# Row maxima copied into the score banks, and the low key products of two tiles side by side

## The chip, the cores and the metric

One core of a Trainium2 chip runs the whole program in one launch. The metric is the time on the device in microseconds (us), as the median of the runs shown.

## The reference

The reference is two small layers on 1024 tokens of width 128 with a context of 6404 rows. The change lies in the first of them, the cross attention. Cut to what matters:

```python
def _L0_xattn_ref(x, latents, ..., Wq, Wkv, Wout):     # 16 heads of 64
    x, lat = layer_norm(x, ...), layer_norm(latents, ...)
    q = lat @ Wq                                       # 1024 queries
    k, v = split(concat([x, lat], axis=1) @ Wkv)       # 6404 + 1024 = 7428 keys
    dots = einsum('bhid,bhjd->bhij', q, k) * scale
    attn = softmax(dots, axis=-1)
    out = einsum('bhij,bhjd->bhid', attn, v)
    return out @ Wout
```

Everything is float32 in the reference. The kernel keeps that accuracy with 16-bit operands: queries, keys, values and probabilities are each held as a high part and a low part, and the products of the parts that matter are added up.

## The kernel before, in words

`stage_attention` takes most of the time. It works head by head (16), for each head over two halves of 512 queries, and in a half over 59 tiles of 128 keys: 58 full ones and a last short one. Two tiles make a unit (30 units a half, 60 a head), and two units, so four tiles, make a period (`PERIODS` = 30 a head, w = 0 to 29). Period 14 holds the last full unit and the short tile of the first half, period 15 begins the second half, and likewise 29 and 0.

For each tile n:

- TensorE (`score`) writes scores, 128 keys by 512 queries, into bank `S[n % 3]`, with two matmuls of 512 columns over all 128 rows. The first multiplies the high keys, held twice (`kc`), with the high and the low part of the queries (`qc`). The second multiplies `kd` with `qd`: its upper 64 rows hold the low keys and the high queries, its lower 64 rows a constant 1/64 and the negated row maximum of the queries, so that the maximum is subtracted inside the matmul.
- ScalarE (`exp`) turns the bank into probabilities in SBUF (one of three buffers of a unit, `prob`), and frees the bank.
- GpSimd (`head` of its block) takes the low part of a whole unit's probabilities, 128 by 1024, into one of three `prob_low`. It waits for both exponentials of the unit and for `low_done` of the unit three earlier.
- TensorE multiplies the high part with the values (`apply_high`: 8 matmuls of 64 or 65 columns a tile) and, two units later, the low part (`apply_low`: 4 matmuls a tile, 8 a unit). All of it adds up in one bank `O`.

Woven into the same order, written out by hand, are two other jobs:

- The maxima of the next head. In each period `window` makes four score products with only 64 rows each (high keys and high queries), in two pairs. The two of a pair stand in different halves of the array. They go to banks `X[0]` to `X[3]`, and VectorE (`take`) reduces them pair by pair to their maxima. A program of 30 windows is offset by 12 periods against the head. Twice a head (w = 13, 27) the maxima of one half are spread over a bank (`spread_top`), and ScalarE writes them negated into `qd` (`place_top`).
- The projections of the next pair of heads. In `side`, TensorE projects 512 columns of queries or keys, or four tiles of values, into `Y`, which is `X[0]`. ScalarE copies the high part out (`copy_task`), VectorE subtracts for the low part (`split_task`), and SyncE writes both to memory, from which whole heads are loaded later (`load_kq`, `load_v`). An even head has 17 such periods (queries and keys: 0, 2, ..., 28 and 9, 19), an odd one 15 (values, all within w = 0 to 22). Heads 14 and 15 have none.

`side` may write `Y` only when the first pair's `take` is done, and the next `window` only when the side's last reader is done (`side_read`). So the order of a projecting period is a loop through bank `X[0]`: window, take, projection, copy, split, window.

In the order of `head` before, a middle period from its window on is: the second tile's `apply_high` of the even unit, a `score`, an `apply_low`; then the odd unit's first `apply_high`, a `score`, the `side`, the second `apply_high`, a `score`, an `apply_low`; then the first `apply_high` of the next period and a `score`, and the next window. Each `score` is three tiles ahead.

Of the kernel before, what the change touches and what calls it, by code (L numbers as in the profile page):

```python
# [18 lines left out]
P = 128  # L19
# [295 lines left out]
def stage_attention(nc, pers, A):  # L315
# [5 lines left out]

    sc = Scope(nc, "att", pers.whole)
    with sc:
# [14 lines left out]
        ident_h = sc.sb("ident_h", [P, P], F16)  # L338
        rden = sc.sb("rden", [P, 4])
# [13 lines left out]
                 "max_scored max_taken top_ready top_spread top_placed inverted normalized tail_ready v_ready kd_ready ident_ready").split()  # L353
# [3 lines left out]
         v_ready, kd_ready, ident_ready) = (s[n] for n in names)  # L357
# [64 lines left out]

        def unit_of(n):
# [14 lines left out]
        def _(sp):  # L438
# [35 lines left out]

            def load_kq(m):
                e = m % 2
                sp.dma_start(kc[0:DH, e, 0:KEYS], k_high[rows(m), :]).then_inc(k_in[e], 16)
                sp.dma_start(kc[DH:P, e, 0:KEYS], k_high[rows(m), :]).then_inc(k_in[e], 16)
                sp.dma_start(qc[0:DH, e, :], q_high[rows(m), :]).then_inc(q_in[e], 16)
                sp.dma_start(qc[DH:P, e, :], q_low[rows(m), :]).then_inc(q_in[e], 16)  # L480
                sp.dma_start(qd[DH:P, e, :], q_high[rows(m), :]).then_inc(q_in[e], 16)
                sp.dma_start(kd[DH:P, e, 0:KEYS], k_low[rows(m), :]).then_inc(k_in[e], 16)

# [18 lines left out]
            sp.dma_start(kd[DH:P, 0, 0:KEYS], k_low[rows(0), :]).then_inc(k_in[0], 16)  # L502
            for b in range(HEADS):
                i, e = divmod(b, 2)
                projecting = i + 1 < HEADS // 2
                for w in range(PERIODS):
                    if w == 0 and b + 1 < HEADS:
                        if b:
                            sp.wait_ge(scored, b * HEAD_TILES)
                        if b and e:  # L510
                            for r in range(NR):
                                sp.wait_ge(kq_out[r], kq_writes(i + 2, r))
                        load_kq(b + 1)
# [74 lines left out]
        def _(pe):  # L588
# [26 lines left out]
            def window(m, e, k, turn):  # L615


                if k == 0:
                    pe.wait_ge(q_in[e], 48 * (turn + 1))
                    pe.wait_ge(k_in[e], 48 * (turn + 1))  # L620
# [29 lines left out]
            def next_score(b, g, i):  # L650
                n = place(b, g, i) + 3
                if n < HEADS * HEAD_TILES:
                    score(n)
# [45 lines left out]
            def side_read(b, e, w, projecting, i):  # L699
# [4 lines left out]
                elif w == BACK_AT:  # L704
                    pe.wait_ge(top_placed, 2 * b + 2)
                elif w == FRONT_AT:
                    pe.wait_ge(top_placed, 2 * b + 3)
# [10 lines left out]
            def head(b, e, with_max, projecting, i):  # L718
                for g in range(UNITS):
                    p, w = g % SIDE, g // 2  # L720
                    if p == 0:
                        next_score(b, g, 0)
                        if g:
                            apply_low(b, e, g - 2)
                        elif b:
                            apply_low(b - 1, 1 - e, LAST - 1)
                        next_window(b, e, w, with_max, projecting, i)
                        if g:
                            apply_low(b, e, g - 1)
                        elif b:  # L730
                            apply_low(b - 1, 1 - e, LAST)
                        next_score(b, g, 1)
                        clear_sums(b, e, g, i)
                        apply_high(b, e, g, 0)
                        apply_high(b, e, g, 1)
                        continue
                    apply_high(b, e, g, 0)
                    next_score(b, g, 0)
                    if g % 2:
                        side(b, e, w, with_max, projecting, i)  # L740
                    else:
                        next_window(b, e, w, with_max, projecting, i)
                    if p < PAIRS:
                        apply_high(b, e, g, 1)
                        next_score(b, g, 1)
                    if p >= 2:
                        apply_low(b, e, g - 2)

# [34 lines left out]
            pe.wait_ge(k_in[0], 48)  # L783
            for n in range(3):
                score(n)
                for x in (66 + 2 * n, 67 + 2 * n):
                    first_slot(x)
# [6 lines left out]
        def _(act):  # L794
# [40 lines left out]

            def head(b, e, with_max, projecting, i):
                for g in range(UNITS):
                    w = g // 2
                    for x, _ in tiles(g):
                        if place(b, g, x) + 3 < HEADS * HEAD_TILES:  # L840
                            exp(place(b, g, x) + 3)
                        n = task_at(e, w) if projecting else None
                        if g % 2 == 0 or x:
                            pass
                        elif n is not None:
                            copy_task(i + 1, n)
                        elif w == BACK_AT:
                            place_top(b, e, 1)
                        elif w == FRONT_AT and with_max:
                            place_top(b + 1, 1 - e, 0)  # L850
# [29 lines left out]
            for n in range(3):  # L880
# [5 lines left out]
        def _(dve):  # L886
# [34 lines left out]

            def finish_max(m, half):
# [13 lines left out]
            def head(b, e, with_max, projecting, i):  # L936
                for w in range(PERIODS):
# [7 lines left out]
                    if n is not None:  # L945
                        split_task(i + 1, n)
                    if 2 * w + 2 in (SIDE, UNITS):
# [787 lines left out]
```

## Time and profile before

| | before |
|---|---|
| median of 3 runs | 2514.27 us (2513.64 to 2515.91) |
| the profiled execution | 2518.84 us, span 2517.0 us |
| TensorE clock granted, mean | 0.98 |
| windows of the maxima, first to last | 122.0 to 2066.1 us of the span |
| TensorE matmul busy | 2375.0 us (94%) |
| GpSimd busy | 1860.1 us (74%) |
| VectorE busy, ScalarE busy | 1580.7 us (63%), 1506.1 us (60%) |

How to read it: the profiled execution is one of its own, 4.57 us above the median of the others, and durations come from it. Its span leaves out what lies around the program. Matmuls are pipelined: a matmul of 512 columns shows a duration of 0.38 us while the next starts 0.215 us after it, so starts are compared, not busy times.

### The profile page before, as it was taken

The numbers are of one execution on the slowest core, as the hardware profiler recorded it, in microseconds if no ns is written. First come the engines' busy times: TensorE is split into PE (matmuls) and PEld (weight loads), VectorE is DVE, ScalarE is ACT, GpSimd is POOL, SyncE is SP. The second block draws the span as 40 slices with busy tenths as digits, with TensorE's granted clock in tenths as the row PEclk, the third lists the DMA queues.
The fourth block names the chain that finished last, engine by engine and source line by source line (L and its number), as shares of the span: only waits on it lengthen the run. The fifth ranks groups of instructions, "written<-read, shape, count | busy, mean of one in ns | idle before, by whom it ended". The sixth has DMA issues, their size and how long they took to land. (4 is left out here: it accounts for less than half of the span.)

```text
span 2517.0 us, 77679 instructions
## 1 busy us (share of the span) xinstructions
PE 2375.0 (94%) x33657; PEld 1488.4 (59%) x33657; DVE 1580.7 (63%) x2342; ACT 1506.1 (60%) x2589; POOL 1860.1 (74%) x1105
## 2 busy tenths in 40 slices
PE   2999999999999999999999999999999998779996
PEld 1355665566556655665566556655665565558884
DVE  8866666666666666666666666666666650467854
ACT  4666666666665666666666666666666665146642
POOL 1788888888888888888888888888889999120001
PEclk9899999999999999999999999999999999889988
DMA  2611323131413141314131413141313000510000
GB/s 86 156 39 45 80 70 103 37 92 61 112 35 90 60 113 40 89 60 113 35 89 64 109 39 90 63 110 38 86 54 99 2 2 7 166 31 2 2 2 12
DMA packets 94102, 162.79 MB, mean 65 GB/s; under 512 B 9976, under 2 KB 83648, under 8 KB 88640
## 3 DMA queue, kind: packets, MB, share of 16 engines
q1 hardware_dynamic: 90464, 153.71, 21.8%
q8 instruction: 265, 4.34, 0.7%
q10 hardware_dynamic: 3296, 4.10, 0.5%
q14 instruction: 77, 0.63, 0.1%
HBM read 95.81 MB, written 61.97 MB: 63 GB/s over the span
## 5 line engine op out<-in xcount | busy, mean ns | idle before, releaser
L581 POOL TENSOR_TENSOR att_prob_low<-att_prob 128x1024 f16<-128x1024 f32 x960 | 1778.7, 1864 | 244.2 <-PE all_banks L683 198.3
L833 ACT ACTIVATE att_prob<-all_banks 128x512 f32<-128x512 f32 x1888 | 1124.0, 597 | 723.4 <-PE all_banks L648 545.0
L915 DVE TENSOR_REDUCE att_part<-all_banks 128x2 f32<-128x1024 f32 x800 | 947.1, 1219 | 419.0 <-PE all_banks L626 419.0
L648 PE MATMUL all_banks<-att_qd,att_kd 128*128 128x512 f16 x1888 | 716.8, 380 | 0.0
L647 PE MATMUL all_banks<-att_qc,att_kc 128*128 128x512 f16 x1888 | 715.8, 379 | 0.0
L670 PE MATMUL all_banks<-att_v,att_prob 128*128 128x65 f16 x7552 | 714.0, 194 | 1.6 <-ACT att_prob L833 0.3
L672 PE MATMUL all_banks<-att_v,att_prob 128*128 128x64 f16 x7552 | 711.8, 195 | 2.2 <-issue 2.2
L670 PEld LDWEIGHTS all_banks<-att_v,att_prob 128*128 128x128 bf16 x7552 | 545.0, 98 | 232.5 <-issue 172.7
L672 PEld LDWEIGHTS all_banks<-att_v,att_prob 128*128 128x128 bf16 x7552 | 536.0, 97 | 42.0
L683 PEld LDWEIGHTS all_banks<-att_v,att_prob_low 128*128 128x128 f16 x7552 | 356.1, 98 | 237.8 <-issue 14.2
L683 PE MATMUL all_banks<-att_v,att_prob_low 128*128 128x65 f16 x7552 | 388.1, 194 | 4.1 <-POOL att_prob_low L581 3.9
L626 PE MATMUL all_banks<-att_kc,att_qc 64*128 64x512 f16 x924 | 272.8, 376 | 13.4 <-DVE att_stage_v L898 6.7
L626 PE MATMUL all_banks<-att_kc,att_qd 64*128 64x512 f16 x924 | 272.8, 376 | 0.0
L647 PEld LDWEIGHTS all_banks<-att_qc,att_kc 128*128 128x128 f16 x1888 | 185.6, 98 | 3.7 <-ACT att_prob L833 3.3
L648 PEld LDWEIGHTS all_banks<-att_qd,att_kd 128*128 128x128 f16 x1888 | 182.4, 97 | 0.0
L626 PEld LDWEIGHTS all_banks<-att_kc,att_qc 64*128 64x128 f16 x924 | 51.3, 94 | 201.2 <-issue 91.5
L1110 POOL MEMSET experts_tie<- 128x1 f32 x64 | 2.3, 98 | 225.6 <-POOLq L1305 195.6
L919 DVE TENSOR_REDUCE att_part<-all_banks 128x1 f32<-128x260 f32 x248 | 126.6, 552 | 52.8 <-PE all_banks L626 52.8
L890 DVE TENSOR_TENSOR att_stage_l<-all_banks,att_stage_h 128x512 f16<-128x512 f32 (+1 forms) x119 | 80.4, 676 | 100.3 <-ACT att_stage_h L797 100.3
L898 DVE TENSOR_TENSOR att_stage_v<-all_banks,att_stage_v 128x256 f16<-128x256 f32 (+1 forms) x210 | 77.5, 411 | 94.5 <-ACT att_stage_v L807 90.2
L1487 DVE TENSOR_TENSOR cross_pt_l<-all_banks,cross_pt_h 128x512 f16<-128x512 f32 (+1 forms) x112 | 70.9, 641 | 36.2 <-ACT cross_pt_h L1437 35.8
L1437 ACT ACTIVATE cross_pt_h<-all_banks 128x512 f16<-128x512 f32 (+1 forms) x112 | 61.2, 555 | 52.6 <-PE all_banks L1578 50.7
(293 smaller groups left out, 2358.5 us busy)
## 6 DMA issues: line engine op xcount, KB each, us to landing
att_kc<-k_high SPq DMA_DIRECT2D x30, 928.5 KB, 10.8
att_v<-v_all SPq DMA_DIRECT2D x14, 1870.5 KB
v_all<-att_stage_v SPq DMA_DIRECT2D x98, 258.0 KB, 2.5
att_kd<-k_low SPq DMA_DIRECT2D x16, 928.5 KB, 15.4
k_high<-att_stage_h SPq DMA_DIRECT2D x98, 128.0 KB, 1.7
k_low<-att_stage_l SPq DMA_DIRECT2D x98, 128.0 KB, 1.9
prep_ctx<-in_ctx SPq DMA_DIRECT2D x5, 640.0 KB, 8.9
later_ctx<-in_ctx SPq DMA_DIRECT2D x1, 3200.0 KB
```

The lines of the kernel that those rows point to most:

```text
L581: pool.tensor_tensor(prob_low[g % NL][:, 0:w], p[:, 0:w], p.bitcast(BF16)[:, 1:2 * w:2], op=ALU.subtract).then_inc(low_split, 1)
L626: pe.matmul(X[x][:, 0:kwidth(c)], q[rows, e, j * P:(j + 1) * P], kc[rows, e, c * BANK:c * BANK + kwidth(c)], start=True, stop=True).then_i ...
L647: pe.matmul(o, kc[:, e, t * P:(t + 1) * P], qc[:, e, q], start=True, stop=False)
L648: pe.matmul(o, kd[:, e, t * P:(t + 1) * P], qd[:, e, q], start=False, stop=True).then_inc(scored, 1)
L670: pe.matmul(O[:, o:o + DH + 1], w, v[:, e, t, 0:DH + 1], start=False, stop=False, skip_group_check=True)
L672: last = pe.matmul(O[:, o:o + DH], w, v[:, e, t, DH + 1:VCOLS], start=False, stop=False, skip_group_check=True)
L683: last = pe.matmul(O[:, o:o + DH + 1], w, v[:, e, t, 0:DH + 1], start=False, stop=True, skip_group_check=True)
L833: act.activation(prob[g % NP][:, i * BANK:(i + 1) * BANK], S[n % 3], ACT.Exp, scale=SCALE)\
L890: dve.tensor_tensor(low[:, 0:w], Y[:, 0:w], high[:, 0:w], op=ALU.subtract).then_inc(y_split, 1)
L898: last = dve.tensor_tensor(st[:, a, 0:w, DH + 1:VCOLS], y, st[:, a, 0:w, 0:DH], op=ALU.subtract)
L915: dve.tensor_reduce(parts[:, n:n + 2], pers.banks[:, 3 + 2 * pair:5 + 2 * pair, :], axis=AX.X, op=ALU.max)\
L919: dve.tensor_reduce(parts[:, n + x:n + x + 1], X[2 * pair + x][:, 0:kwidth((n + x) % K_CHUNKS)], axis=AX.X, op=ALU.max).then_inc(max_taken, 1)
```

## The change

In 26 of the 30 periods of a head (all but w = 0, 14, 15 and 29) two of the four tiles are scored in another way. Tiles n+2 and n+3 of the period are called seeded here:

- The negated maxima of a half are now also kept as a 128 by 512 array in SBUF (`nm`), by a second ScalarE instruction in `place_top`.
- ScalarE copies `nm` into the bank of tile n+3 right behind the exponential of tile n, which frees that bank, and ahead of the exponential of n+1 (`seed` in the ScalarE block). VectorE copies `nm` into the bank of tile n+2 at the end of its period's work, behind `split_task`.
- TensorE (`low_pair`) then adds the low keys times the high queries with two matmuls of 64 rows, one in each half of the array, and then the two high products of 128 rows (`high_scores`). So seven slots of 512 columns, one of them shared by two matmuls of half height, stand in place of eight for the four tiles' scores.
- For the lower half of the array, the low keys of 13 tiles (6, 10, ..., 54) are loaded over the constant in `kd[0:64]` (`load_upper`: 64 rows of 13 pieces of 256 bytes, once a head).
- The order of TensorE's period is rewritten: window, low pair, two high products, the even unit's two `apply_high`, the `side`, a `score`, an `apply_low`, an `apply_high`, a `score`, an `apply_high`, an `apply_low`. A `score` is now two to three tiles ahead. At the start of a half both late `apply_low` stand ahead of the window.

```diff
+            def load_upper(m):
+                s = k_low[rows(m), 0:FULL_TILES * P].rearrange("p (t c) -> p t c", c=P)[:, 6:FULL_TILES - 2:4, :]
+                o = kd[0:DH, m % 2, 0:FULL_TILES * P].rearrange("p (t c) -> p t c", c=P)[:, 6:FULL_TILES - 2:4, :]
+                sp.dma_start(o, s).then_inc(k_in[m % 2], 16)
...
+            def low_pair(n, u):
...
+                pe.wait_ge(even_seeded, u + 1)
+                pe.matmul(S[n % 3], kd[0:DH, e, t * P:(t + 1) * P], qc[0:DH, e, q], start=False, stop=False,
+                          skip_group_check=True)
+                pe.wait_ge(odd_seeded, u + 1)
+                pe.matmul(S[(n + 1) % 3], kd[DH:P, e, (t + 1) * P:(t + 2) * P], qd[DH:P, e, q], start=False, stop=False,
+                          skip_group_check=True)
...
+                for w in range(PERIODS):
+                    g, n, u = 2 * w, place(b, 2 * w), seeds_before(b, w)
...
+                    if first:
+                        score(n + 2)
+                        if n:
+                            apply_low(*((b, e, g - 2) if g else (b - 1, 1 - e, LAST - 1)))
+                            apply_low(*((b, e, g - 1) if g else (b - 1, 1 - e, LAST)))
+                    next_window(b, e, w, with_max, projecting, i)
+                    if u is not None:
+                        low_pair(n + 2, u)
+                        high_scores(n + 2)
+                        high_scores(n + 3)
+                    elif last:
+                        score(n + 2)
+                    else:
+                        score(n + 3)
                         clear_sums(b, e, g, i)
                     apply_high(b, e, g, 0)
+                    apply_high(b, e, g, 1)
+                    side(b, e, w, with_max, projecting, i)
+                    if after < HEADS * HEAD_TILES:
+                        score(after)
+                    if not first:
                         apply_low(b, e, g - 2)
+                    apply_high(b, e, g + 1, 0)
+                    if after < HEADS * HEAD_TILES:
+                        score(after + 1)
+                    if not last:
+                        apply_high(b, e, g + 1, 1)
+                    if not first:
+                        apply_low(b, e, g - 1)
...
+                act.activation(nm[:, half, :], Y, ACT.Copy, scale=-1.0, bias=LIFT).then_inc(nm_placed, 1)
...
+                act.activation(S[n % 3], nm[:, g // SIDE, :], ACT.Copy).then_inc(odd_seeded, 1)
...
+                    if after < HEADS * HEAD_TILES:
+                        exp(after)
+                        u = seeds_before(*next_period(b, w))
+                        if u is not None:
+                            seed(after + 3, u)
+                        exp(after + 1)
...
+                dve.tensor_copy(S[n % 3], nm[:, g // SIDE, :]).then_inc(even_seeded, 1)
```

## Rows read from the trace of the kernel before

**Rows 1.** The page: busy time, share of the span and instructions of each engine.
```profile
PE 2375.0 (94%) x33657; PEld 1488.4 (59%) x33657; DVE 1580.7 (63%) x2342; ACT 1506.1 (60%) x2589; POOL 1860.1 (74%) x1105
```
**Rows 2.** Windows: length, busy time of each engine, granted clock, DMA share, GB/s.
```profile
1000.00:2000.00 1000.00, 986.56 (x14997) 597.42 (x14996) 640.19 (x765) 629.62 (x1069) 880.99 (x476) 1.00 0.26 72
```
**Rows 3.** The page's costliest groups: busy, mean ns of one, idle before and releaser.
```profile
L581 POOL TENSOR_TENSOR att_prob_low<-att_prob 128x1024 f16<-128x1024 f32 x960 | 1778.7, 1864 | 244.2 <-PE all_banks L683 198.3
L833 ACT ACTIVATE att_prob<-all_banks 128x512 f32<-128x512 f32 x1888 | 1124.0, 597 | 723.4 <-PE all_banks L648 545.0
L915 DVE TENSOR_REDUCE att_part<-all_banks 128x2 f32<-128x1024 f32 x800 | 947.1, 1219 | 419.0 <-PE all_banks L626 419.0
```
**Rows 4.** Timeline, TensorE in a plain period of head 14 (start, length).
```profile
1981.31 0.39 PE L626 MATMUL all_banks<-att_kc,att_qc 64*128 64x512 f16 x1
...
1982.10 0.38 PE L647 MATMUL all_banks<-att_qc,att_kc 128*128 128x512 f16 x1
...
1982.53 0.41 PE L683 MATMUL all_banks<-att_v,att_prob_low 128*128 128x65 f16 x8
...
1983.03 0.38 PE L647 MATMUL all_banks<-att_qc,att_kc 128*128 128x512 f16 x1
...
1985.15 0.39 PE L626 MATMUL all_banks<-att_kc,att_qc 64*128 64x512 f16 x1
```
**Rows 5.** Timeline of period 4 of head 8, which projects keys, and the next window.
```profile
1159.73 0.39 PE L626 MATMUL all_banks<-att_kc,att_qc 64*128 64x512 f16 x1
...
1161.88 0.38 PE L594 MATMUL all_banks<-shared_kvh,shared_wk_h 128*128 128x512 f16 x1
...
1162.31 0.38 PE L596 MATMUL all_banks<-shared_kvh,shared_wk_l 128*128 128x512 f16 x1
...
1162.79 0.60 ACT L797 ACTIVATE att_stage_h<-all_banks 128x512 f16<-128x512 f32 x1
...
1163.41 0.69 DVE L890 TENSOR_TENSOR att_stage_l<-all_banks,att_stage_h 128x512 f16<-128x512 f32 x1 [1.06 <-ACT att_stage_h L797]
...
1164.22 0.39 PE L626 MATMUL all_banks<-att_kc,att_qc 64*128 64x512 f16 x1
...
1164.75 2.35 DVE L915 TENSOR_REDUCE att_part<-all_banks 128x2 f32<-128x1024 f32 x2 [0.65 <-PE all_banks L626]
```
**Rows 6.** Timeline: two exponentials of head 8 that follow each other.
```profile
1166.58 1.27 ACT L833 ACTIVATE att_prob<-all_banks 128x512 f32<-128x512 f32 x2 [0.33 <-PE all_banks L648]
```
**Rows 7.** Timeline of period 7 of head 9, which projects values.
```profile
1304.32 0.39 PE L626 MATMUL all_banks<-att_kc,att_qc 64*128 64x512 f16 x1
...
1307.98 0.75 DVE L898 TENSOR_TENSOR att_stage_v<-all_banks,att_stage_v 128x256 f16<-128x256 f32 x2 [0.78 <-ACT att_stage_v L807]
...
1308.84 0.28 PE L626 MATMUL all_banks<-att_kc,att_qc 64*128 64x260 f16 x1
```
**Rows 8.** Timeline, head 9: first matmuls of the windows of periods 14, 15, 16.
```profile
1334.16 0.39 PE L626 MATMUL all_banks<-att_kc,att_qc 64*128 64x512 f16 x1
...
1337.33 0.39 PE L626 MATMUL all_banks<-att_kc,att_qc 64*128 64x512 f16 x1
...
1342.53 0.39 PE L626 MATMUL all_banks<-att_kc,att_qc 64*128 64x512 f16 x1
```
**Rows 9.** Timeline of GpSimd: two units of head 9, and 15 of head 14.
```profile
1394.09 3.75 POOL L581 TENSOR_TENSOR att_prob_low<-att_prob 128x1024 f16<-128x1024 f32 x2 [0.33 <-PE all_banks L683]
...
1971.56 28.81 POOL L581 TENSOR_TENSOR att_prob_low<-att_prob 128x1024 f16<-128x1024 f32 x15 [0.47 <-PE all_banks L683]
```
**Rows 10.** Timeline: windows 1 and 2 of head 9, just behind its loads.
```profile
1274.64 0.39 PE L626 MATMUL all_banks<-att_kc,att_qc 64*128 64x512 f16 x1
...
1282.08 0.60 PE L626 MATMUL all_banks<-att_kc,att_qc 64*128 64x512 f16 x1
```
**Rows 11.** The page, DMA queue: packets, MB, share of 16 engines.
```profile
q1 hardware_dynamic: 90464, 153.71, 21.8%
```

More of the change, by code:

```diff
@@ L482, in load_kq @@
                 sp.dma_start(kd[DH:P, e, 0:KEYS], k_low[rows(m), :]).then_inc(k_in[e], 16)
+                load_upper(m)
             def load_v(m):
@@ L502, in _ @@
             sp.dma_start(kd[DH:P, 0, 0:KEYS], k_low[rows(0), :]).then_inc(k_in[0], 16)
+            sp.wait_ge(kd_ready, 1)
+            load_upper(0)
             for b in range(HEADS):
@@ L512, in _ @@
                                 sp.wait_ge(kq_out[r], kq_writes(i + 2, r))
+                        if b == 0:
+                            sp.wait_ge(filled, 1)
                         load_kq(b + 1)
@@ L619, in window @@
                     pe.wait_ge(q_in[e], 48 * (turn + 1))
-                    pe.wait_ge(k_in[e], 48 * (turn + 1))
+                    pe.wait_ge(k_in[e], 64 * (turn + 1))
                 for x in range(WINDOW):
@@ L718, in head @@
             def head(b, e, with_max, projecting, i):
[L719 to L732, printed above, removed]
+                for w in range(PERIODS):
+                    g, n, u = 2 * w, place(b, 2 * w), seeds_before(b, w)
+                    first, last = g % SIDE == 0, g % SIDE == PAIRS - 1
+                    after = place(b, g + 1) + len(tiles(g + 1))
+                    if first:
[12 more added lines that the diff above has]
+                        score(n + 3)
@@ L782, in _ @@
             pe.wait_ge(q_in[0], 48)
[L783 to L787, printed above, removed]
+            pe.wait_ge(k_in[0], 64)
+            score(0)
+            for x in range(66, 69):
+                first_slot(x)
+            score(1)
+            for x in range(69, EARLY):
+                first_slot(x)
+            pe.wait_ge(nm_placed, 1)
             for b in range(HEADS):
@@ L834, in exp, with seed @@
                    .then_inc(exp_done, 1)
-            def head(b, e, with_max, projecting, i):
[L837 to L850, printed above, removed]
+            def seed(n, u):
+                b, g, _ = unit_of(n)
+                act.wait_ge(nm_placed, 2 * b + g // SIDE + 1)
+                act.wait_ge(exp_done, EXP0 + n - 2)
+                act.activation(S[n % 3], nm[:, g // SIDE, :], ACT.Copy).then_inc(odd_seeded, 1)
+            def head(b, e, with_max, projecting, i):
+                for w in range(PERIODS):
+                    last = 2 * w % SIDE == PAIRS - 1
+                    n, after = place(b, 2 * w), place(b, 2 * w + 1) + len(tiles(2 * w + 1))
+                    exp(n + 2)
+                    if not last:
+                        exp(n + 3)
+                    t = task_at(e, w) if projecting else None
+                    if t is not None:
+                        copy_task(i + 1, t)
+                    elif w == BACK_AT:
+                        place_top(b, e, 1)
+                    elif w == FRONT_AT and with_max:
+                        place_top(b + 1, 1 - e, 0)
+                    if after < HEADS * HEAD_TILES:
[4 more added lines that the diff above has]
+                        exp(after + 1)
             act.wait_ge(constants, 1)
@@ L879, in _ @@
                 act.wait_ge(first_out[r], 16 * len(range(r, KQ_TASKS, NF)))
-            for n in range(3):
+            for n in range(2):
                 exp(n)
@@ L946, in head @@
                         split_task(i + 1, n)
+                    u = seeds_before(*next_period(b, w))
+                    if u is not None and (w + 1 < PERIODS or with_max):
+                        seed(place(b, 2 * w + 1) + len(tiles(2 * w + 1)) + 2, u)
                     if 2 * w + 2 in (SIDE, UNITS):
```

48 lines of the change are left out of this document (26 added, 22 removed).

## The prediction

> **What bounds the kernel now.** Look first at the busy shares [rows 1] and then at the long middle of the attention [rows 2]: TensorE is busy 98.7% of it, at the full clock of 2.4 GHz (granted 1.00), GpSimd 88%, VectorE 64%, ScalarE 63%. In the costliest groups [rows 3], GpSimd and VectorE idle mostly "until TensorE", which is what a TensorE-bound loop looks like from the side.
>
> Busy shares don't say how dense a pipelined TensorE is, so I compare starts. In a plain period [rows 4] two matmuls of 512 columns lie between 1982.10 and 1982.53, 0.215 us each, and sixteen small ones between 1982.53 and 1983.03, 0.25 us for eight. From a window's first matmul to the next product of 128 rows are 0.54 us (0.79 less one `apply_high` of 0.25). Eight large matmuls (1.72), six groups of eight small ones (1.50) and the window (0.54) make 3.76; the period is 3.84. The 0.08 left is a gap just ahead of the window. The window itself is two pairs of 0.215, so it has another gap of 0.11 behind it. There is no other hole: a plain period is pure TensorE work, and what leaves TensorE's order can shorten it.
>
> A period that projects keys [rows 5] is 4.49: the same and 3 x 0.215. One that projects values [rows 7] is 4.52. GpSimd needs two units a period. Two that follow each other without a wait take 3.75 with the first at 1.89, so a unit costs 1.86 and a period 3.72 [rows 9]. In head 14 fifteen units follow each other at 28.81 - 1.89 over 14 = 1.92, 3.85 a period: GpSimd there runs at TensorE's pace with only 0.13 in hand. That is the ceiling to keep in mind.
>
> **The change, part by part.**
>
> *The saving.* 416 of 480 periods are seeded (26 x 16). In each, two low products of 0.215 become one pair. The window shows what a pair costs: two pairs lie in its 0.43, so 0.215 a pair. It stands right behind the window, so the gap of 0.11 is paid once for both. That takes 0.215 off: 3.63 for a plain period. The Trainium skill, TensorEngine Tiling (Array Packing), Key Properties, says that changing the tiling mode drains TensorE; by that rule too the pair is cheap only beside the window. The trace agrees with its 0.08 and 0.11 on the two sides of each window.
>
> *The side's wait (the main loss).* Before, the projection starts 2.15 after its window (1159.73 to 1161.88) [rows 5]. In the new order TensorE reaches it after window and pair, 0.43 + 0.215, gap 0.10, two high products 0.43 and two `apply_high` 0.50: 1.68. But it must wait for the first `take`. That starts 0.53 behind the window (1164.22 to 1164.75) and lasts 1.22 [rows 3]; a wait of TensorE on VectorE costs about 0.12 more (split ends 1163.41 + 0.69 = 1164.10, window 1164.22). So the projection can start at 1.87, 0.19 late. Then 0.65 of projection, 1.84 of the rest (two `score` 0.86, two `apply_high` and two `apply_low` 1.00) and the gap of 0.09: a period of 4.45 or 4.46. Against 4.49 and 4.52 this leaves 0.035 with keys and 0.06 with values. 15 x 7 = 105 key periods and 13 x 7 = 91 value periods are seeded: 3.7 + 5.0 = about 9 us of the 42 that their low products are worth.
>
> *The rest of the loop through the bank.* The copy starts 0.91 after the projection (1161.88 to 1162.79): 2.78, ends 3.38; the split 0.69 ends at 4.10, with values (two, 0.75) [rows 7] at about 4.2. The next window needs it 0.12 later, at most 4.3, before 4.46. It does not bind.
>
> *The seeds.* No row has a copy of 128 x 512 into a bank. For ScalarE the nearest are 0.597 and 0.60 for the same size out of a bank [rows 3, 5]; for VectorE the subtraction of 0.69 above and half of the reduction, 0.61. I take 0.6 for both, with ends 0.4 and 1.2 (a whole reduction). VectorE's seed follows the split: in place at 4.10 to 4.2 + 0.6 + 0.12 = 4.8 to 4.95. The pair is due at 4.46 + 0.43 = 4.89. The few hundredths with values vanish in the 0.19 of the side's wait. At 1.2 the seed is 0.4 to 0.6 late. ScalarE starts an instruction every 0.67 (1.27 - 0.60) [rows 6]: exponential n+2 at 1.17, n+3 at 1.84, copy 2.78, n+4 3.45, seed 4.12 to 4.72, in place at 4.84, just in time; n+5 ends at 5.4, and it is wanted no earlier than 1.4 into the next period. In plain periods all of this is earlier by the copy's turn. ScalarE's six turns are 4.0 of 4.46. So the seeds are hidden, by 0.05 plus the 0.19.
>
> *Plain periods.* 26 x 14 = 364 seeded ones of heads 0 to 13, less 196 with a projection, less 28 that spread maxima, leave 140 at 0.215: 30 us. GpSimd wants 3.72 against 3.63, a lag of 0.09 a period. What its lateness meets first is the exponential of the next unit, which needs the probabilities' buffer of three units before; that is due some 1.4 us after GpSimd has finished with it. So about 15 plain periods in a row can pass before it binds, and in these heads projecting periods of 4.46 lie between. In heads 14 and 15, 35 seeded plain periods have a window (24 and 11): 7.5 us. The 15 at and after the end of head 15's windows are GpSimd's already and give nothing.
>
> *Spreading.* `spread_top` waits for the same `take`: the period becomes 4.04 against 4.08 by the same sum, 29 times 0.04, 1 us. ScalarE makes two copies there; behind w = 27 the seed is then some 0.35 late where no projection covers it, 7 times, -2.5 us.
>
> *The ends of the halves.* Value heads take 3.17 and 5.20 for periods 14 and 15 [rows 8], where dense TensorE work would be 7.6: waits for GpSimd's last unit, for the sums' normalization and for `take` behind it. In the new order both late `apply_low` come before the window, and the window covers more of the normalization; but VectorE's `take` is behind it as before. By my sum the periods come out 0.1 to 0.2 longer where the second one projects, and 0.4 to 0.7 shorter elsewhere. I count nothing, with ends -8 and +8 us over 31 ends.
>
> *The load.* `load_upper` adds 832 pieces, 0.21 MB, 15 times in the loop. The queue's 90464 packets took 21.8% of 16 engines' span, 97 ns each on average [rows 11]: by packets 5 us of all 16 engines, by bytes 0.8. The key tiles come early enough. But value writes queue behind it at the start of odd heads, where periods already stretch to 7.44 [rows 10]. I take 0.4 in each of 7 heads, 3 us; the ends are 0 and 14. The beginning, with fewer slots ahead of the first head, I count at nothing.
>
> Sum: 9 + 30 + 7.5 + 1 - 2.5 - 3 = 42 us. On the profiled execution, 2518.84 gives 2477; it lies 4.6 above the median of the runs, so the forecast is 2514.3 - 42, about 2473.
>
> **The rivals.**
>
> *GpSimd sets the plain periods* (0.12). If its slack is smaller than I read, a plain period is 3.72: 175 x 0.09 = 15 us less gain, 2488. For it: the fifteen units without a break [rows 9]. Against: it idles in projecting periods.
>
> *The whole saving* (0.08). If the first `take` is in time, the projecting periods gain 0.215 too, 196 x 0.17 = 33 us more: 2440. It needs `take` to begin 0.2 earlier, which nothing here does.
>
> *Late seeds* (0.15, the slower side). The place is the first wait of `low_pair`: behind it queue both high products, so both exponentials and GpSimd's unit. In projecting periods the seed may be about 0.2 later than I reckon for nothing; from there each 0.1 costs 20 us over 196 periods, and at 0.4 late the gain of 42 is gone. A VectorE copy of 1.0 decides it; at 1.2 the time is near 2549, and with 0.3 beyond the slack on both engines 2532.
>
> *No side by side* (0.09). The pair's second matmul stands behind a wait of its own, which the window's pairs don't have. If that splits them, nothing is saved in plain periods and the forecast's small terms remain: about 2517. If the pair were also drained for apart from the window, by the skill's rule in TensorEngine Tiling, the two gaps of 0.19 come on top. In rows of this case: 416 x 0.19 = 79 us, about 2596 and slower; of the 0.09 this has 0.02.
>
> *The ends and the load at their bad ends* (0.06): 8 + 11 us less, 2492.
>
> **How the numbers follow.** The forecast's own case has 0.50 and a range of 2460 to 2488. About 0.2% (5 us) is what a measurement of this kernel can tell from no change. Faster: 0.50 + 0.12 + 0.08 + 0.06 = 0.76, and I add nothing. Late seeds are slower, 0.15, and of no side by side I give 0.06 to no change and 0.03 to slower: 0.18 slower, 0.06 same. The range for 8 in 10 reaches from the whole saving, 2440, to 2512, where seeds a little late still lie.
>
> **What would show it.** In the changed kernel's timeline, a plain period from window to window should be 3.63 to 3.65 and a projecting one 4.46, with the projection 1.87 behind its window and TensorE's idle time before L594 ended by `take`. The two matmuls of the pair should start within a few hundredths of each other, 0.43 behind the window. GpSimd should show units in unbroken rows with short waits. A copy by VectorE over 0.8 us, waits for `nm` copies ahead of the pair above 0.2 us, or plain periods at 3.85 would prove me wrong.

## The result and the profile after

| | before | after |
|---|---|---|
| median | 2515.09 us (2513.64 to 2520.87) | 2497.73 us (2495.17 to 2501.99) |
| ratio | | 0.9929 [0.9916, 0.9942] |
| the profiled execution | 2518.84 us, span 2517.0 | 2501.99 us, span 2500.1 |
| windows of the maxima, first to last | 122.0 to 2066.1 us | 121.0 to 2045.7 us |

The kernel is faster by 17.4 us, 0.7%. The forecast was 42 us. The direction held, and so did the wide range of 2440 to 2512; the forecast's own range of 2460 to 2488 was missed, and the size is off by more than half.

The page's busy times, three of its costliest groups and its queue row, which answer to [rows 1, 3, 11]:

```profile
PE 2336.5 (93%) x33657; PEld 1532.4 (61%) x33657; DVE 1830.6 (73%) x2758; ACT 1675.0 (67%) x3037; POOL 1848.4 (74%) x1105
...
q1 hardware_dynamic: 104032, 157.12, 22.9%
...
L607 POOL TENSOR_TENSOR att_prob_low<-att_prob 128x1024 f16<-128x1024 f32 x960 | 1767.0, 1868 | 239.2 <-PE all_banks L723 145.2
L986 DVE CAST all_banks<-att_nm 128x512 f32<-128x512 f16 x416 | 284.3, 684 | 39.3 <-ACT att_prob L880 38.8
L888 ACT ACTIVATE all_banks<-att_nm 128x512 f32<-128x512 f16 x416 | 250.4, 602 | 38.5 <-ACT att_prob L880 0.4
```

The seeds cost 0.68 and 0.60 us, near the 0.6 of the forecast. The queue carries 13568 packets more and only 3.41 MB more. A line of the windows view of the middle (length, busy PE, PEld, DVE, ACT, POOL, granted clock, DMA share, GB/s) is the surprise:

```profile
1000.00:1900.00 900.00, 876.56 (x13530) 562.65 (x13528) 692.01 (x888) 643.49 (x1167) 785.81 (x428) 0.99 0.29 78
```

GpSimd does 428 instructions in these 900 us where the kernel before does 424 in the same stretch: 0.9% more, though plain periods are over 5% shorter (below). And TensorE, 98.7% busy before [rows 2], is now 97.4%. Holes have appeared. A plain period first, then a hole; the timeline gives start, length, engine, line:

```profile
1226.30 0.39 PE L652 MATMUL all_banks<-att_kc,att_qc 64*128 64x512 f16 x1
1226.74 0.38 PE L682 MATMUL all_banks<-att_qc,att_kd 64*128 64x512 f16 x1
1226.74 0.38 PE L685 MATMUL all_banks<-att_qd,att_kd 64*128 64x512 f16 x1
1227.05 0.60 PE L692 MATMUL all_banks<-att_qc,att_kc 128*128 128x512 f16 x2
...
1229.93 0.39 PE L652 MATMUL all_banks<-att_kc,att_qc 64*128 64x512 f16 x1
```

From window to window are 3.63 us, as forecast, against 3.84 [rows 4]. The pair's two matmuls start at the same hundredth, 0.44 behind the window. So the change does what it says. The hole, in head 8, just behind its loads:

```profile
1134.11 0.39 PE L652 MATMUL all_banks<-att_kc,att_qc 64*128 64x512 f16 x1
...
1135.20 1.82 SPq L508 DMA_DIRECT2D att_v<-v_all  x1
...
1140.17 3.03 SPq L467 DMA_DIRECT2D q_low<-att_stage_l  x1
...
1150.19 0.39 PE L652 MATMUL all_banks<-att_kc,att_qc 64*128 64x512 f16 x1
...
1156.38 0.60 ACT L843 ACTIVATE att_stage_h<-all_banks 128x512 f16<-128x512 f32 x1 [3.92 <-DMA q_low<-att_stage_l]
...
1157.01 0.69 DVE L949 TENSOR_TENSOR att_stage_l<-all_banks,att_stage_h 128x512 f16<-128x512 f32 x1 [4.20 <-ACT att_stage_h L843]
...
1157.76 0.61 PE L652 MATMUL all_banks<-att_kc,att_qc 64*128 64x512 f16 x1 [3.22 <-DVE att_stage_l L949]
```

Read it from the bottom. The window at 1157.76 comes 7.57 after the one at 1150.19, since it waits for the split, the split for the copy, and the copy for a DMA: `q_low`, the write of the first projection of this head, issued at 1140.17. There are two stage buffers, so the third copy (w = 4) can't start before the first buffer's writes have landed, and these stand in the queue behind the loads that the head issues at its start. Before, the same copy came at 1162.79 [rows 5] and waited for no more than 0.2 us at its worst. The waits view says how often (total us, times, longest). After:

```profile
ACT att_stage_h L843 <- DMA q_low<-att_stage_l: 21.5, 6, 4.1
ACT att_stage_v L853 <- DMA v_all<-att_stage_v: 19.7, 7, 3.9
```

Before:

```profile
ACT att_stage_v L807 <- DMA v_all<-att_stage_v: 8.3, 6, 2.5
ACT att_stage_h L797 <- DMA q_low<-att_stage_l: 0.2, 1, 0.2
```

The stall costs more than its length. The windows view (columns as above), head 8:

```profile
1150.00:1158.00 8.00, 4.78 (x74) 2.97 (x72) 3.18 (x6) 3.30 (x7) 4.94 (x3) 0.91 0.62 245
1158.00:1164.00 6.00, 6.00 (x60) 3.27 (x56) 3.35 (x4) 3.32 (x7) 3.40 (x2) 0.55 0.15 48
```

Behind the hole the granted clock is 0.55, which is near the lower of the two levels (1.2 GHz), and the window's matmul takes 0.61 instead of 0.39. The plain period that begins at 1157.76 lasts 6.25. Not every stall is followed by that: in head 13 the stalled period lasts 6.91, and the next one 4.48 at the full clock.

### The profile page after: what moved, and what is told of

The parts are those of the page before. It is cut to its first block and busy times, and to the rows that moved or that the text cites. A ratio compares the mean times of both kernels' runs of the same rounds, so it can differ in the third digit from the quotient of the medians.

```text
span 2500.1 us, 79392 instructions
## 1 busy us (share of the span) xinstructions
PE 2336.5 (93%) x33657; PEld 1532.4 (61%) x33657; DVE 1830.6 (73%) x2758; ACT 1675.0 (67%) x3037; POOL 1848.4 (74%) x1105
## 5 line engine op out<-in xcount | busy, mean ns | idle before, releaser
L880 ACT ACTIVATE att_prob<-all_banks 128x512 f32<-128x512 f32 x1888 | 1071.0, 591 | 380.8 <-PE all_banks L692 253.1
L712 PE MATMUL all_banks<-att_v,att_prob 128*128 128x64 f16 x7552 | 660.7, 195 | 0.1
L710 PE MATMUL all_banks<-att_v,att_prob 128*128 128x65 f16 x7552 | 658.5, 193 | 0.8 <-issue 0.5
L723 PEld LDWEIGHTS all_banks<-att_v,att_prob_low 128*128 128x128 f16 x7552 | 329.1, 98 | 136.5 <-POOL att_prob_low L607 14.7
L673 PE MATMUL all_banks<-att_qc,att_kc 128*128 128x512 f16 x1056 | 403.8, 382 | 0.0
L674 PE MATMUL all_banks<-att_qd,att_kd 128*128 128x512 f16 x1056 | 403.3, 382 | 0.0
L723 PE MATMUL all_banks<-att_v,att_prob_low 128*128 128x65 f16 x7552 | 386.8, 194 | 10.2 <-POOL att_prob_low L607 8.0
L986 DVE CAST all_banks<-att_nm 128x512 f32<-128x512 f16 x416 | 284.3, 684 | 39.3 <-ACT att_prob L880 38.8
L652 PE MATMUL all_banks<-att_kc,att_qc 64*128 64x512 f16 x924 | 274.0, 377 | 33.6 <-DVE att_stage_l L949 17.3
L888 ACT ACTIVATE all_banks<-att_nm 128x512 f32<-128x512 f16 x416 | 250.4, 602 | 38.5 <-ACT att_prob L880 0.4
L692 PE MATMUL all_banks<-att_qc,att_kc 128*128 128x512 f16 x832 | 255.1, 389 | 0.0
L685 PE MATMUL all_banks<-att_qd,att_kd 64*128 64x512 f16 x416 | 158.6, 381 | 1.1
L682 PE MATMUL all_banks<-att_qc,att_kd 64*128 64x512 f16 x416 | 158.4, 381 | 0.9 <-issue 0.9
L692 PEld LDWEIGHTS all_banks<-att_qc,att_kc 128*128 128x128 f16 x832 | 47.3, 97 | 152.2 <-issue 152.2
## 6 DMA issues: line engine op xcount, KB each, us to landing
att_kc<-k_high SPq DMA_DIRECT2D x30, 928.5 KB, 10.7
att_v<-v_all SPq DMA_DIRECT2D x14, 1870.5 KB
att_kd<-k_low SPq DMA_DIRECT2D x16, 928.5 KB, 15.1
```

The lines of the kernel that those rows point to most:

```text
L652: pe.matmul(X[x][:, 0:kwidth(c)], q[rows, e, j * P:(j + 1) * P], kc[rows, e, c * BANK:c * BANK + kwidth(c)], start=True, stop=True).then_i ...
L673: pe.matmul(o, kc[:, e, t * P:(t + 1) * P], qc[:, e, q], start=True, stop=False)
L674: pe.matmul(o, kd[:, e, t * P:(t + 1) * P], qd[:, e, q], start=False, stop=True).then_inc(scored, 1)
L692: pe.matmul(S[n % 3], kc[:, e, t * P:(t + 1) * P], qc[:, e, h * HALF:(h + 1) * HALF], start=False, stop=True, skip_group_check=True).then_ ...
L710: pe.matmul(O[:, o:o + DH + 1], w, v[:, e, t, 0:DH + 1], start=False, stop=False, skip_group_check=True)
L712: last = pe.matmul(O[:, o:o + DH], w, v[:, e, t, DH + 1:VCOLS], start=False, stop=False, skip_group_check=True)
```

## The experiments

Each experiment edits either the changed kernel or the kernel before. Ratios are to the kernel before as timed beside each: 2513.63 us beside experiments 1 to 4, 2515.60 beside 5 to 8, 2515.91 beside 9 and 10. So a difference between experiments of two groups is known to some 2 us. The intervals of the ratios reach 3 to 6 us to either side.

### 1. Without the new load

```diff
-                load_upper(m)
...
-            sp.wait_ge(kd_ready, 1)
-            load_upper(0)
...
-                    pe.wait_ge(k_in[e], 64 * (turn + 1))
+                    pe.wait_ge(k_in[e], 48 * (turn + 1))
```

> The changed kernel without the loads of the low keys' second copy, so the lower half of the array multiplies the old constant for 13 tiles a head (that part of the scores is another number; every instruction of the engines stays). Theory A (the loads of a head are a fixed stretch of about 20 us, TensorE now arrives at the fifth period earlier, and the new load adds about 1.5 us to the stretch): the stalls of periods 3 to 5 shrink by about 1.8 us in each even and 1.3 us in each odd head, 7 of each, some 22 us: 2476. Theory B (the new load alone is what was lost, 5 us a pair of heads): 2463. Rival C (the stalls come from the seeds, not from the queue): no change, 2497.

Measured: 2471.39 us, 0.9833 [0.9813, 0.9852]. The gain is 42.2 us instead of 17.4: 0.21 MB a head cost 24.9 us, give or take some 6 by the two intervals. The time lies between theory A's 2476 and theory B's 2463, nearer to A; rival C is out. The stall is shorter and not gone:

```profile
ACT att_stage_h L840 <- DMA q_low<-att_stage_l: 14.4, 6, 2.8
ACT att_stage_v L850 <- DMA v_all<-att_stage_v: 11.7, 7, 3.0
```

Periods 4 and 5 of the even heads last 5.78 and 4.23 on average, against 6.80 and 5.26 with the load. The gain here equals the forecast's 42 by luck: two errors cancel (below).

### 2. The kernel before with the new load

```diff
+                load_upper(m)
...
-                    pe.wait_ge(k_in[e], 48 * (turn + 1))
+                    pe.wait_ge(k_in[e], 64 * (turn + 1))
```

> The kernel before with only the new load added (it overwrites the constant for 13 tiles a head, so the maxima are subtracted wrongly there; nothing else differs). Theory A: even heads had no slack (the write landed 0.06 us before its buffer was wanted), so the added 1.5 to 1.8 us is a stall at once, and odd heads give about 1.3: some 20 us over 7 pairs, 2535. If the load is hidden, as the prediction had it but for 3 us: 2515 to 2518.

Measured: 2528.28 us, 1.0059 [1.0037, 1.0082], 14.7 us slower than its 2513.63, where theory A had 20 and a hidden load 4 at most. The load costs the old kernel six tenths of what it costs the new one: its waits are 4.3 us for `q_low` and 15.8 for `v_all`. So the load is not a fixed price; it falls due where the slack is gone.

### 3 and 4. The head's loads spread, in both kernels

The key and query loads go out in four steps at chosen periods in place of one burst at w = 0, and the value load of an even head's period 0 at w = 12. In the changed kernel the new load goes with the fourth step. Nothing is computed differently. In both:

```diff
+                    if projecting:
+                        at = (0, 2, 5, 8) if e else (1, 3, 5, 7)
+                        if w in at:
+                            load_kq(b + 1, at.index(w))
+                        if b and not e and w == 12:
+                            sp.wait_ge(low_done, LOW0 + b * UNITS)
+                            load_v(b + 1)
```

> The changed kernel with the loads of the next head issued in four steps over the first nine periods instead of all at its start (even heads: periods 1, 3, 5, 7 and the values at 12; odd heads: 0, 2, 5, 8). Same bytes and pieces. Theory A: the stalls of periods 3 to 5 vanish, 4.0 us in an even and 3.3 us in an odd head, 7 of each, 51 us: 2447. Theory B gives the same or less, since the pieces are still there: 2447 to 2475. Rival C: 2497.

> The kernel before with its loads issued in the same four steps. Its stalls behind the loads are 1.9 us in each of 7 odd heads and none in even ones: about 13 us, 2501. If the loads' burst costs it nothing: 2514.

Measured: the changed kernel 2448.08 us, 0.9735 [0.9719, 0.975]; the kernel before 2503.71 us, 0.9959 [0.9943, 0.9975]. The first is what theory A of experiment 3 had (2447), the second 3 us above its forecast. With the queue out of the way the change itself is worth 2503.71 - 2448.08 = 55.6 us. The waits for `q_low` and `v_all` are gone from the first; an even head's first write lands 6.5 to 8.4 us after the head's first window instead of 21.8 to 22.4. A projecting period, now undisturbed:

```profile
1202.14 0.39 PE L664 MATMUL all_banks<-att_kc,att_qc 64*128 64x512 f16 x1
1202.67 2.36 DVE L986 TENSOR_REDUCE att_part<-all_banks 128x2 f32<-128x1024 f32 x2 [0.98 <-PE all_banks L664]
1203.95 0.39 PE L632 MATMUL all_banks<-shared_kvh,shared_wk_h 128*128 128x512 f16 x1
...
1206.55 0.39 PE L664 MATMUL all_banks<-att_kc,att_qc 64*128 64x512 f16 x1
```

The projection starts 1.81 behind the window, the period is 4.41; with values it is 4.43. The reduction begins 0.53 behind the window, as before. In the periods whose window starts with a narrow pair (w = 4, 8 and 19 with keys, 4 and 19 with values) the first `take` is shorter, the projection starts 1.69 behind the window, and the period lasts 4.28 to 4.30: more evidence that the side waits for `take`.

### 5. Both: loads spread, and the late low product ahead of the side

If TensorE waits for `take` at the side, work that is not behind it could fill the wait.

```diff
                     apply_high(b, e, g, 1)
+                    if not first:
+                        apply_low(b, e, g - 2)
                     side(b, e, w, with_max, projecting, i)
                     if after < HEADS * HEAD_TILES:
                         score(after)
-                    if not first:
-                        apply_low(b, e, g - 2)
```

> The changed kernel with its loads spread as before and one step of TensorE's order moved: the even unit's late low product (0.25 us) stands ahead of the side instead of behind the next score. Theory A (the projection waits for the first take, 0.13 us in the trace, and the loop through the bank has room): a key period falls from 4.41 to about 4.28, a value period from 4.43 to 4.35 (there the loop copy, split, window comes out at 4.35): 105 x 0.13 + 91 x 0.08 = 21 us, 2427. Rival (the projecting period is held by something else, the seeds or the exponentials): 2448.

Measured: 2446.24 us, 0.9725 [0.9706, 0.9743], only 1.8 us under experiment 3, where 21 were expected; it is the rival's 2448 that came. Projecting periods behind a plain one did shrink, to 4.28 with keys and 4.30 with values; behind another projecting one they stayed at 4.39 and 4.44. What was gained in one period was paid in the next. TensorE's wait for VectorE's seed, here, and in experiment 3:

```profile
PEld all_banks L694 <- DVE all_banks L998: 93.6, 220, 0.5
```

```profile
PEld all_banks L694 <- DVE all_banks L998: 48.1, 213, 0.5
```

Plain periods behind a projecting one now last 3.745 instead of 3.635, and their low pair starts 0.54 to 0.56 behind the window instead of 0.44. (In experiment 3 the wait of the weight loads lies in the shadow of the window's matmuls: the pair starts at 0.44 there.) The seed is behind the split on VectorE, and the shorter the period, the later it is: the next experiment of this line is number 10.

### 6. The pair apart from the window

On experiment 3: one `apply_high` (eight small matmuls of 128 rows) is put between the window and the pair, so TensorE changes between 64 and 128 rows twice more.

```diff
                     if u is not None:
+                        apply_high(b, e, g, 0)
                         low_pair(n + 2, u)
...
-                    apply_high(b, e, g, 0)
+                    if u is None:
+                        apply_high(b, e, g, 0)
```

> The changed kernel with its loads spread and the low pair moved one step away from the window: the first high product with the values (0.25 us) stands between them. If each switch between 64 and 128 rows costs its gap (0.08 and 0.11 us beside every window), a plain period rises from 3.63 to 3.82, and a projecting one, where 0.13 of it hides in the wait for take, by 0.06: 175 x 0.19 + 196 x 0.06 = 45 us, 2493. If the gaps beside the window come from its waits and not from the switch: 2448.

Measured: 2504.25 us, 0.9953 [0.9938, 0.9968], 56 us above experiment 3 and 11 more than expected. The plain period is 3.84, 0.21 longer with the same matmuls; projecting periods and those that spread maxima grow by about 0.09. The two matmuls of the pair still start together (the window's first pair, its second, the last small matmul, the pair, the high products):

```profile
1200.40 0.39 PE L664 MATMUL all_banks<-att_kc,att_qc 64*128 64x512 f16 x1
...
1200.63 0.38 PE L664 MATMUL all_banks<-att_kc,att_qc 64*128 64x512 f16 x1
...
1201.17 0.19 PE L724 MATMUL all_banks<-att_v,att_prob 128*128 128x64 f16 x1
1201.30 0.39 PE L694 MATMUL all_banks<-att_qc,att_kd 64*128 64x512 f16 x1
1201.30 0.39 PE L697 MATMUL all_banks<-att_qd,att_kd 64*128 64x512 f16 x1
1201.62 0.60 PE L704 MATMUL all_banks<-att_qc,att_kc 128*128 128x512 f16 x2
```

The pair has 0.13 from the last small matmul's start to its own, where small ones follow each other every 0.03, and 0.32 from its start to the next product, where a pair costs 0.215: a gap of 0.10 on each side. No wait stands in TensorE's order between the pair and the high products, so the gap behind it comes with the change of rows. The place beside the window is worth as much as the pairing itself. The forecast's price for the two changes, 0.08 + 0.11, was right within 0.02.

### 7. Both matmuls in one half of the array

```diff
-                pe.matmul(S[n % 3], kd[0:DH, e, t * P:(t + 1) * P], qc[0:DH, e, q], start=False, stop=False,
+                pe.matmul(S[n % 3], kd[DH:P, e, t * P:(t + 1) * P], qd[DH:P, e, q], start=False, stop=False,
```

> The changed kernel with its loads spread and both matmuls of the low pair in the upper half of the array (the low keys stand there for every tile, so the numbers are the same). It takes the running side by side away and leaves everything else. Theory A: a plain period rises by 0.215 to 3.85, a projecting one by 0.08 (the rest hides in the wait for take): 175 x 0.215 + 196 x 0.08 = 53 us, 2501. If the pair is not the source of the saving: 2448.

Measured: 2501.37 us, 0.994 [0.9925, 0.9956], where 2501 was expected. The two now start one after the other:

```profile
1199.86 0.38 PE L694 MATMUL all_banks<-att_qd,att_kd 64*128 64x512 f16 x1
1200.08 0.38 PE L697 MATMUL all_banks<-att_qd,att_kd 64*128 64x512 f16 x1
```

The plain period is 3.85, the key period 4.50, the value period 4.52: the numbers of the kernel before [rows 4, 5, 7] within 0.01. Without the shared slot 53 of the change's 55.6 us are gone.

### 8. A longer seed on VectorE

A copy of half the size is put ahead of VectorE's seed.

```diff
+                dve.tensor_copy(S[n % 3][:, 0:HALF // 2], nm[:, g // SIDE, 0:HALF // 2]).then_inc(seeded_once, 1)
+                dve.wait_ge(seeded_once, u + 1)
                 dve.tensor_copy(S[n % 3], nm[:, g // SIDE, :]).then_inc(even_seeded, 1)
```

> The changed kernel with its loads spread and VectorE's seed made longer: it first copies half of the columns, waits for that, and then all of them, some 0.45 us more (a seed of 1.1 us in all). By the prediction's sum the seed of a projecting period is then 0.45 late, 0.13 of which hides in the wait for take: 196 x 0.32 = 63 us, 2511; plain periods have just enough room. If the seeds have more room than that: 2448 to 2470.

Measured: 2514.01 us, 0.9991 [0.9981, 1.0], 66 us above experiment 3 and 3 above what was expected. The seed takes 1.15 us in all (0.42, 0.70 and the wait between), and with it the whole gain is gone. The place was not as I had it: it is the period behind a projecting one that grows. Plain ones there last 3.96, key periods 4.61 and value periods 4.65; projecting periods behind a plain one stay at 4.41 and 4.43. In the ones that grow the pair starts 0.76 to 0.78 behind the window instead of 0.44, since it meets the late seed:

```profile
PEld all_banks L695 <- DVE all_banks L1001: 162.6, 268, 1.0
```

### 9. The new load late

On the changed kernel, with the old burst as it is: `load_upper` alone moves from the burst to w = 8.

```diff
-                load_upper(m)
...
+                    if w == 8 and b + 1 < HEADS:
+                        load_upper(b + 1)
```

> The changed kernel with one edit: the new load of a head is issued in its ninth period instead of behind the other loads at its start. Everything else, the other loads' burst too, stays. Theory A: the same as without the new load, 2471, because only its place in the queue ahead of the writes costs anything. If its 832 pieces cost something wherever they stand: nearer to 2497.

Measured: 2472.57 us, 0.9829 [0.9806, 0.9852], the same as with no new load at all (2471.39). Same pieces, same bytes, 25 us less: its place in the queue is the cost, and its transfer costs nothing that these two intervals, 5 us to either side, can tell.

### 10. Experiment 5 with the seed ahead of the split

```diff
-                    if n is not None:
-                        split_task(i + 1, n)
                     u = seeds_before(*next_period(b, w))
...
+                    if n is not None:
+                        split_task(i + 1, n)
```

> The kernel with the loads spread and the late low product ahead of the side, with VectorE's seed ahead of its split. There a projecting period had fallen from 4.41 to 4.28, but the next plain one had risen from 3.63 to 3.75, with TensorE waiting for the seed. If the seed behind the split is what holds it, plain periods return to 3.63; the split then ends at 4.25 with keys and 4.33 with values and holds the next window at 4.37 and 4.45: a key period and a plain one are 8.00 against 8.03, about 2446, no gain. If the copy and not VectorE is late, the plain period stays at 3.75 and the whole becomes slower, 2460.

Measured: 2422.16 us, 0.9628 [0.9613, 0.9642], the best version, 76 us under the changed kernel. That is 24 us under the nearer of the two expectations. Its middle, and its wait for the seed:

```profile
1000.00:1900.00 900.00, 893.89 (x14167) 588.82 (x14165) 719.47 (x916) 673.32 (x1220) 826.69 (x451) 1.00 0.27 77
```

```profile
PEld all_banks L694 <- DVE all_banks L998: 3.1, 10, 0.3
```

I had reckoned that the split would then end too late for the window. The timeline shows that the seed runs while ScalarE is still copying:

```profile
1178.43 0.39 PE L664 MATMUL all_banks<-att_kc,att_qd 64*128 64x512 f16 x1
1181.23 0.68 DVE L998 CAST all_banks<-att_nm 128x512 f32<-128x512 f16 x1
1181.27 0.60 ACT L855 ACTIVATE att_stage_h<-all_banks 128x512 f16<-128x512 f32 x1 [0.58 <-PE all_banks L634]
1181.90 0.69 DVE L961 TENSOR_TENSOR att_stage_l<-all_banks,att_stage_h 128x512 f16<-128x512 f32 x1
1182.71 0.28 PE L664 MATMUL all_banks<-att_kc,att_qc 64*128 64x260 f16 x1
```

Copy and seed end together at 1181.9, so the split loses nothing and the period is 4.28, with plain ones back at 3.635.

## Why the forecast was right in direction and off in size

**Plain periods: right.** 3.635 against the forecast 3.63, and experiments 6 and 7 show both parts of its reason: the pair in one slot (0.215) and its place beside the window (0.21). The drain rule of the Trainium skill (TensorEngine Tiling (Array Packing), Key Properties) fits experiment 6 with its 0.21; the case in which it would have made the change slower did not come, because the pair stands right behind the window, at 0.44 with two pairs of 0.215 before it, so without a gap.

**Projecting periods: right mechanism, a little better.** The side waits for the first `take`: 1.81 behind the window (forecast 1.87), periods 4.41 and 4.43 (4.46; its rest of the period, 0.86 + 1.00, is 1.86 and not the 1.84 that the sum has). Against the old kernel's 4.50 and 4.52 this is 105 x 0.09 + 91 x 0.09 = 18 us where I had 9, and 21 with the periods whose window starts with a narrow pair (experiments 3 and 4, period by period). Experiment 5 shows that the wait could be filled, but the seed has to come first.

**Spreading and w = 28: right or a little better.** 3.985 (4.04); the seed behind w = 27 in odd heads costs 3.75 - 3.63 = 0.12, not 0.35.

**Ends of the halves: the sum held.** In value heads periods 14 and 15 take 8.56 together against 8.36 [rows 8], in key heads 8.00 against 8.76. I counted nothing and kept 8 either way; all the periods 0, 14, 15 and 29 together are 2.3 us shorter in experiment 3 than in experiment 4.

**Seeds: right in size, with the wrong place for their lateness.** 0.68 and 0.60, and the pair starts 0.44 behind the window in nearly all periods; in the first seeded one of a half it is up to 0.16 late, behind w = 27 its second matmul 0.12. Experiment 8 bears out that a longer copy eats the gain, at 1.15 us; at the "1.0" of the forecast nothing was run. The lateness shows in the period behind a projecting one, not in the projecting one.

**GpSimd: right for the plain periods, wrong for head 15.** It does not set the plain periods, at 3.63 or in experiment 10; in head 14 TensorE waits for it three times, 0.8 us at the longest. But the forecast counted the 11 plain periods of head 15 that have a window as gain (2.4 us). They are 3.4 us shorter (39.4 against 42.9), and what follows the last window until the last low product is 3.1 us longer (72.8 against 69.7, in the changed kernel and the one before). GpSimd works there almost without a break in both, so what TensorE gains ahead of it is given back.

**The step that failed: "The load".** I put it at 3 us, in 7 odd heads only, with ends 0 and 14. It is 24.9 us (experiments 1 and 9). Three things are wrong in it. I looked at value writes alone, and took the key copy at 1162.79 [rows 5] as an example of a copy without a wait, while the `q_low` write it needs had landed at 1162.73, 0.06 earlier (0.02 to 0.81 in the six even heads that have such a write). Nor was the 7.44 of [rows 10] a wait for a write: in that period TensorE idles for 2.22 us with no releaser in the profile, and no other odd head has such a period 1. What the value writes stretch is period 3, to 5.0 to 7.0 us in the other six odd heads. The line of the timeline before:

```profile
1280.86 0.22 PE L672 MATMUL all_banks<-att_v,att_prob 128*128 128x64 f16 x1 [2.22 <-issue]
```

Further, I priced the load by its 5 us of all engines, when what counts is that every write behind it lands later: after 21.8 to 22.4 us from an even head's first window with it, 20.4 to 21.1 without. (The moment of issue is not what counts: in the kernel before the write is issued 5.6 us after the window and lands at 19.7 to 20.6; without the new load it is issued at 4.6 and lands at 20.4 to 21.1.) And I did not see that the shortening of the periods itself moves the third copy forward against the same burst: it is wanted 18.7 us after the head's first window now and came at 20.5 to 20.7 before. This last part hits the kernel without any new load too: 13.4 us (below), for which the sum has no term.

The account: the change with its loads spread gives 55.6 us, where the forecast without its load term is 45. The traces of experiments 3 and 4, which are 58.4 apart, show by kind of period where the rest comes from: projecting periods 12 us more than forecast, spreading and w = 28 some 3, the ends and the beginning 4, less 3 or 4 for the plain periods and 3 for what follows the last window. So the 45 was also low, by 10 to 13 from several small terms, and experiment 1's 42.2 is near the forecast's 42 by luck. Of the 55.6, the new load in the burst takes 24.9. The old burst takes 2471.39 - 2448.08 = 23.3, of which the kernel before paid 2513.6 - 2503.71 = 9.9 too, so 13.4 are new. 55.6 - 24.9 - 13.4 = 17.3 is the gain again; the parts are differences of the same runs, so that they add up proves nothing, but each part is a measurement.

How much of the load's price is the wait and how much the lower clock? TensorE's own idle time that ended with a split is 17.3 + 13.9 us in the changed kernel and 10.2 + 6.3 without the new load, 14.7 less; with the loads spread there is none. After, and experiment 1:

```profile
PE all_banks L652 <- DVE att_stage_l L949: 17.3, 6, 3.4
PE all_banks L652 <- DVE att_stage_v L957: 13.9, 7, 3.1
```

```profile
PE all_banks L649 <- DVE att_stage_l L946: 10.2, 6, 2.1
PE all_banks L649 <- DVE att_stage_v L954: 6.3, 5, 2.2
```

The time at less than the full clock, as span times one less the mean granted clock, is 68 us in the changed kernel (mean of its four runs, 0.970 to 0.975), 52 in experiment 1 (0.978 to 0.979) and 48 in experiment 3 (0.980 to 0.981). That is an estimate, since some of it falls into the holes themselves. By it about half of the 24.9 us is the wait for the writes, and about half is the lower clock that followed nine of the thirteen stalls.

## What to carry to other kernels

When a change shortens the loop, look for every wait that is now almost met, even those that show zero idle time: a copy that comes 0.06 us after the write that frees its buffer is a stall once the loop before it is 1.8 us shorter. Price a new DMA by what stands behind it in its queue and when that is wanted, not by its bytes, and put it where nothing is due: here the same load cost 25 us in one place and nothing in another. And where two engines' work meets at one buffer, put on the second engine whatever fits into the first one's time: the seed under ScalarE's copy turned 2 us of gain into 26.

## What the runs showed of the hardware that I had not expected

- A write issued 6 us after a head's first window (1140.17) let its reader start 16 us later (1156.38), behind loads of about 5 MB (by the page, 3 x 928.5 KB of keys, 208 of the new load, 3 x 128 of queries, 1870.5 of values); with the loads spread, such writes land 6.5 to 8.4 us after that window.
- 832 pieces of 256 bytes in that burst delay the write behind them by 1.3 us on average (0.9 to 2.0 over 13 heads, changed kernel against experiment 1).
- In head 8 a hole of 3.2 us in TensorE is followed by 6 us at a granted clock of 0.55. Shorter ones can be followed by it too: head 11's hole of 1.8 us, not head 13's of 2.4.
- Two more changes between 64 and 128 rows cost about 0.21 us, with eight small matmuls between (experiment 6).
- A copy of 128 x 512 from half precision into a bank costs VectorE 0.68 and ScalarE 0.60 us.
